# One-core decoder layer with routed experts: the last group's routing, tile tables and scatters spread over more tiles

## The chip, the core and the metric

The kernel runs on one core of one Trainium2 chip. The metric is the time of the whole kernel on the device in microseconds (us), the median of several runs.

## What is computed

Sixteen sequences of 128 tokens with 128 features pass three sublayers, each followed by an addition and a layer norm: a self-attention with circulant projections, a cross attention with a context of 120 rows, and a mixture-of-experts layer. Only the last one matters here. In the reference it is

```python
scores = jax.nn.softmax(xt @ gate_w.T, axis=-1)
_, idx = jax.lax.top_k(scores + gate_b, 2)
...
for each of the 8 experts:
    h = swiglu((xt @ ew1 + eb1) * (xt @ ew3 + eb3))
    routed = routed + ce[:, None] * (h @ ew2 + eb2)
shared = swiglu((xt @ sw1 + sb1) * (xt @ sw3 + sb3)) @ sw2 + sb2
return routed + shared
```

(the loop is a scan in the reference). So each of the 2048 tokens goes to two of eight experts, and to one shared expert.

## The kernel before, in words

**Stages.** The sixteen batches are four groups of four (`NG`, `G4`). A long software pipeline of slots (`front`, slots up to `LAST_SLOT`) does the attentions. For groups 0 to 2 it also does the routing. From iteration m = -1 on a second pipeline runs 47 expert tiles of 128 rows through the experts (`tile`, lines 1471, 845 and 1067): tiles 0 to 7 are the shared expert for the last eight batches, tiles 8 to 23 (`NE` = 16) hold rows of groups 0 to 2 sorted by expert, and tiles 24 to 46 the rest, with the last group's rows in them. From m = 6 on only this tile pipeline is left, and all that is changed lies in it.

**A routed row's way.** GpSimd scatters each token's row twice into the DRAM buffer `xs` at the place `slot` (`scatter`, L628; before the fourth and the eighth batch's half `mark`, L615, writes destination and weight beside the rows). SyncE loads one tile of 128 rows from `xs` into a ring of four buffers (`load`, L471) by an address that it reads from the table `row_of`. TensorE transposes it. The products follow, ScalarE scales the result with the row's weight (L868), and GpSimd places it in the DRAM buffer `ys` (`place`, L706) by destinations that `meta` (L690) took out of the loaded rows. After all tiles `ys` is read back and summed, normed and stored.

**One iteration m of the tile pipeline.** TensorE (L1520, L1551 to L1560) transposes the hidden values of tile m-2 and the input rows of tile m+1 (L1482, L1484), makes the first product of tile m (L1491 into pS), the down product of tile m-2 (L1502 into pM) and the second product of tile m (L1491 into pT). It starts with a wait for the hidden values of tile m-2. VectorE's loop m does whatever routing is due, and then tile m-1: product (L1071), two clips (L1073, L1074), gate (L1076), hidden (L1079). ScalarE copies, takes a tanh and scales the output of tile m-2. GpSimd calls `place(i)` when the output of routed tile i is there, in iteration m = i + 10, then `meta(i + 4)`.

**The last group's routing** is written by hand into VectorE's loops. It has nine steps: 0 the largest logit, 1 softmax and bias, 2 and 3 the first choice, 4 and 5 the second, 6 the weights, 7 first rows (after two small matmuls of counts on TensorE, `counts`, L1359), 8 the slots. Then come `late_tiles` (eleven small instructions) and `tile_table` (seven), which give `expert_of` and `row_of` for tiles 24 to 46. Nearly every one of them goes through `link`, which makes the next one wait for its end. `LAST_ROUTING` names the loop of each step: steps 1 and 2 in loop 7, 3 and 4 in loop 8, 5 in loop 9, 6 and 7 in loop 10, 8 in loop 11. `LAST_COUNT` = 10, `LAST_TILES` = 12, `LAST_TABLE` = 13.

**The last group's scatters** are eight, in two batches of four: behind `place(1)` and `meta(5)`, and behind `place(3)` and `meta(7)` (L722). GpSimd works in order.

**SyncE** loads routed tiles 0 to 15 (numbered r, tile r + 8), each once the ring's buffer is free (`t_ps`, `meta_sb`). Behind `load(9)` (`PAD_LOAD`) it writes eight blocks of padding rows, one for each expert. Then it waits for all eight scatters of the last group, the padding and the second table, and goes on with `load(16)`, which TensorE reads in iteration 23:

```python
sp.wait_ge(s_scat_last, 16 * 2 * G4)
sp.wait_ge(s_pad, 16 * (E + 1))
sp.wait_ge(tab_sb, 2)
for r in range(NE, NR):
    load(r)
```

Of the kernel before, what the change touches and what calls it, by code (L numbers as in the profile page):

```python
# [22 lines left out]
G4 = 4  # L23
NG = B // G4
# [10 lines left out]
NR = (2 * B * P + E * (P - 1)) // P  # L35
NE = (2 * (NG - 1) * G4 * P - E * (P - 1)) // P
# [9 lines left out]
X_SLOTS = {-7: 1, 1: 2, 9: 3}  # L46
BIAS_SLOTS = {7: 0, 11: 1, 15: 2}
SHARED_SLOT, SHARED_SLOTS, SHARED_DOWN = 25, 20, 9
PAD_LOAD = 9
LAST_ROUTING = {6: (0,), 7: (1, 2), 8: (3, 4), 9: (5,), 10: (6, 7), 11: (8,)}  # L50
LAST_COUNT, LAST_TILES, LAST_TABLE = 10, 12, 13
RING = 4
XW = D + 2
CAP = B * P + P
# [13 lines left out]
def decoder_layer(nc, x, ctx_1024, wq_c, wq_b, wk_c, wk_b, wv_c, wv_b, wo_c, wo_b, w_sim, b_sim, W_qv, b_qv,  # L68
# [9 lines left out]
    with ctx:  # L78
# [291 lines left out]
        def scat_sem(g):  # L370
            return s_scat_last if g == NG - 1 else s_scat
# [6 lines left out]
        def _(sp):  # L378
# [92 lines left out]
            def load(r):  # L471

                row = sp.value_load(row_of[0:1, bass.ds(r, 1)], min_val=0, max_val=DUMMY)
                if r >= RING:
                    sp.wait_ge(t_ps, NA + r - RING + 1)
                    sp.wait_ge(meta_sb, r - RING + 1)
                sp.dma_start(XR[:, r % RING, :], xs.ap()[bass.ds(row, P), :]).then_inc(s_load[r % RING], 16)
# [53 lines left out]
            for r in range(NE):  # L531
                load(r)
                if r == PAD_LOAD:
                    sp.wait_ge(pad_sb, 1)
# [26 lines left out]
        def _(pool):  # L561
# [53 lines left out]
            def mark(g, k):  # L615

                if k == 0:
                    pool.wait_ge(slots_sb, g + 1)
                    pool.wait_ge(x2_sb, G4 * (g + 1))
                else:  # L620
                    pool.wait_ge(scat_sem(g), 16 * G4 * (2 * g + 1 if g < NG - 1 else 1))
                rows = X2[:, g * G4:(g + 1) * G4, :]
                pool.tensor_copy(rows[:, :, D:D + 1].rearrange("p b o -> p (b o)"), dest[:, k, g * G4:(g + 1) * G4])
                pool.tensor_copy(rows[:, :, D + 1:D + 2].rearrange("p b o -> p (b o)"),
                                 weight[:, k, g * G4:(g + 1) * G4]).then_inc(marked, 1)
                pool.wait_ge(marked, 2 * g + k + 1)

            def scatter(g, i):  # L628

                k, b = i // G4, g * G4 + i % G4  # L630
                if i % G4 == 0:
                    mark(g, k)
                pool.indirect_dma_start(xs.ap(), bass.IndirectOffsetOnAxis(ap=slot[:, k, b:b + 1], axis=0),  # L633
                                        X2[:, b, :], None).then_inc(scat_sem(g), 16)
# [55 lines left out]
            def meta(i):  # L690

                k = i % (2 * RING)
                pool.wait_ge(s_load[i % RING], 16 * (i // RING + 1))
                if i >= 2 * RING:
                    pool.wait_ge(s_ysc[i % RING], 16 * (i // RING - 1))
                pool.tensor_tensor(row_weight[:, k:k + 1], XR[:, i % RING, D + 1:D + 2], zero[:], ALU.add)
                to = XR[:, i % RING, D:D + 1]
                if i % RING == 0:
                    pool.tensor_copy(row_dest[:, k:k + 1], to).then_inc(meta_sb, 1)
                else:  # L700

                    pool.tensor_scalar(spare[:, k:k + 1], to, 2.0 * TOKENS - 0.5, float(i % RING * P), ALU.is_ge, ALU.mult).then_inc(spare_sb, 1)
                    pool.wait_ge(spare_sb, i - i // RING)
                    pool.tensor_scalar(row_dest[:, k:k + 1], spare[:, k:k + 1], to, None, ALU.add).then_inc(meta_sb, 1)

            def place(i):  # L706

                k = i % (2 * RING)
                pool.wait_ge(y_sb, NA + 1 + i)
                pool.wait_ge(meta_sb, i + 1)  # L710
                pool.indirect_dma_start(ys.ap(), bass.IndirectOffsetOnAxis(ap=row_dest[:, k:k + 1], axis=0),  # L711
                                        YO[:, i % RING, :], None).then_inc(s_ysc[i % RING], 16)
# [5 lines left out]
            for i in range(NR):  # L718
                place(i)
                if i + RING < NR:  # L720
                    meta(i + RING)
                if i in (1, 3):  # L722
                    for k in range(G4):
                        scatter(NG - 1, (i // 2) * G4 + k)
            for g in range(NG):
                here = slice(g * G4, (g + 1) * G4)
                mean, var = (meanvar3[:, here, i:i + 1].rearrange("p b o -> p (b o)") for i in range(2))
# [11 lines left out]
        def _(act):  # L739
# [153 lines left out]
            for m in range(LAST_SLOT - FFN_SLOT + 1, NT + 2):  # L893
                if 0 in LAST_ROUTING.get(m, ()):
                    route_exp(NG - 1)
# [11 lines left out]
        def _(dve):  # L907
# [176 lines left out]
            def link(ins):  # L1084

                steps_done[0] += 1
                ins.then_inc(rt, 1)
                dve.wait_ge(rt, steps_done[0])
# [69 lines left out]
            def first_tiles():  # L1158

                link(dve.tensor_tensor_scan(tiles_cum[:], ones[:, 0:E], tiles[:], 0.0, ALU.mult, ALU.add))  # L1160
                link(dve.tensor_tensor(total[:], tiles_cum[:], tiles[:], ALU.subtract))
                link(dve.memset(start[:, E:E + 1], float(DUMMY)))
                link(dve.scalar_tensor_tensor(out=start[:, 0:E], in0=total[:], scalar=float(-P), in1=region[:], op0=ALU.mult, op1=ALU.add))
# [7 lines left out]
                link(dve.tensor_scalar(used[:], used[:], 0.0, None, ALU.max))  # L1171
                link(dve.tensor_tensor(step[:], start[:, 1:E + 1], start[:, 0:E], ALU.subtract))

            def late_tiles():

                round_tiles((P - 1) / (2.0 * P))
                link(dve.tensor_tensor(tiles[:], tiles[:], used[:], ALU.subtract))
                first_tiles()
                link(dve.scalar_tensor_tensor(out=start[:, 0:E], in0=used[:], scalar=float(P), in1=start[:, 0:E], op0=ALU.mult, op1=ALU.add))
                link(dve.tensor_tensor(step[:], start[:, 1:E + 1], start[:, 0:E], ALU.subtract))  # L1180

            def tile_table(first, n):


                link(dve.tensor_tensor(past[:, 0:n], iota_t[:, 0:n].rearrange("p (t o) -> p t o", o=1).to_broadcast([1, n, E]),
                                       bass.AP(tiles_cum, 0, [[E, 1], [0, n], [1, E]]), ALU.is_ge))
                link(dve.tensor_reduce(out=tab_f[:, 0:n], in_=past[:, 0:n], axis=AX.X, op=ALU.add))
                link(dve.tensor_scalar(expert_of[:, NA + first:NA + first + n], tab_f[:, 0:n], float(E - 1), None, ALU.min))
                link(dve.tensor_tensor(past_step[:, 0:n], past[:, 0:n], bass.AP(step, 0, [[E, 1], [0, n], [1, E]]), ALU.mult))
                link(dve.tensor_reduce(out=row_f[:, 0:n], in_=past_step[:, 0:n], axis=AX.X, op=ALU.add))  # L1190
                link(dve.scalar_tensor_tensor(out=row_f[:, 0:n], in0=row_f[:, 0:n], scalar=start[0:1, 0:1], in1=iota_rows[:, 0:n],
                                              op0=ALU.add, op1=ALU.add))
                dve.tensor_scalar(row_of[:, first:first + n], row_f[:, 0:n], float(DUMMY), None, ALU.min).then_inc(tab_sb, 1)
# [36 lines left out]
            for n in range(FIRST_SLOT, LAST_SLOT + 1):  # L1230
                if n == PREP_SLOT:
                    dve.wait_ge(s_small, 16 * SMALL)
                    for q in range(4):
                        context(q)
                front(n)
                for g in range(NG - 1):
                    if n == G4 * U * g + ROUTE_SLOT and g == 0:
                        dve.wait_ge(c_pool, 4)
                    routing(g, n - G4 * U * g - ROUTE_SLOT)
                if shared_use(n - 1):  # L1240
                    shared_products(*shared_use(n - 1))
                if shared_use(n - 2):
                    shared_hidden(*shared_use(n - 2))
                if n == EARLY_TILES:
                    early_tiles()
                if n == EARLY_TILES + 1:
                    tile_table(0, NE)
                if n >= FFN_SLOT + 1:
                    tile(n - FFN_SLOT - 1, (n - FFN_SLOT - 1) % 2)
            for m in range(LAST_SLOT - FFN_SLOT + 1, NT + 1):  # L1250

                for k in LAST_ROUTING.get(m, ()):
                    routing(NG - 1, k)
                    if k == LATE_COUNT + 1:
                        padding_rows()
                if m == LAST_TILES:
                    late_tiles()
                if m == LAST_TABLE:
                    tile_table(NE, NR - NE)
                tile(m - 1, (m - 1) % 2)  # L1260
            for g in range(NG):
                final_stats(g)
# [338 lines left out]
```

## Time and profile before

| what | us |
|---|---|
| median of 3 runs | 420.73 |
| lowest and highest of them | 417.86, 422.58 |
| the profiled execution | 423.07 |
| its span, first to last instruction | 421.3 |

The rows below are of the profiled execution. Times are from the start of its span. PE is TensorE's matmul, DVE is VectorE, ACT ScalarE, POOL GpSimd, SPq the issuing of SyncE. A name such as L1482 is a line of the kernel before. A bracket at the end of a row gives the idle time before it and what ended it. The first iteration of the tile pipeline whose transposed rows come from `xs` (shown as sim_add) is iteration 7; the L1482 row then marks the start of each iteration.

### The profile page before, as it was taken

The page shows a single profiled execution, that of the slowest core. Times are in us where ns is not written, and L with a number is a line of the kernel's source. Part 1 is how long each engine was busy: PE and PEld are TensorE (multiplying, and loading weights), DVE is VectorE, ACT ScalarE, POOL GpSimd, SP SyncE. Part 2 cuts the span into 40 slices and gives each one's busy share as a digit, 9 for nine tenths or more (in the row PEclk, how much of TensorE's full clock was granted, in tenths as well). Part 3 has the DMA queues.
Part 4 walks back from the last instruction along what each step waited for, and adds up shares of the span by engine and source line. Part 5 has one row for each costly group of instructions (what it writes and reads, how often), then busy time and mean ns, then how long its engine had stood idle before and what let it go on. Part 6 is the DMA issues. An engine that isn't in the chain of part 4 may idle for free.

```text
span 421.3 us, 8518 instructions
## 1 busy us (share of the span) xinstructions
PE 347.6 (82%) x2415; PEld 224.6 (53%) x2415; DVE 281.5 (67%) x834; ACT 175.3 (42%) x498; POOL 194.0 (46%) x377
## 2 busy tenths in 40 slices
PE   2637887888988879798967998978799999999880
PEld 1224466666656658576656554534455555555450
DVE  3435477777878897869876867987466666666322
ACT  2212344444534443344532344344355555555313
POOL 9700022224222558722474434357755656565323
PEclk9999999998999998969998799999899999999996
DMA  4764544766654732310003001113211111110063
GB/s 100 171 212 128 178 141 120 210 202 172 186 157 132 201 98 63 104 34 11 27 28 119 14 13 44 33 39 92 63 45 44 47 45 45 40 50 19 26 201 100
DMA packets 53197, 39.56 MB, mean 94 GB/s; under 512 B 7623, under 2 KB 46632, under 8 KB 53147
## 3 DMA queue, kind: packets, MB, share of 16 engines
q1 hardware_dynamic: 50881, 34.33, 29.3%
q0 software_dynamic: 2272, 4.69, 3.3%
q8 instruction: 22, 0.36, 0.4%
q14 instruction: 22, 0.18, 0.1%
HBM read 26.05 MB, written 12.69 MB: 92 GB/s over the span
## 4 chain that ended last, share of the span: by engine, by line
PE 42%; DVE 23%; issue 10%; POOL 9%; DMA 6%; SPq 5%; ACT 2%; ACTq 0%; POOLq 0%; DVEq 0%
PE pT L1491 7%; PE pS L1491 6%; DVE negmax L934 4%; PE pM L1502 4%; POOL xs L633 3%; PE pM L1297 3%; DVE inv_den L950 2%; POOL rstd L613 2%; PE pO L1482 2%; PE pT L1321 2%; PE pT L1492 2%; PE pS L1311 2%; PE pS L1492 2%; PE pO L1334 2%; DVE X L1004 1%
## 5 line engine op out<-in xcount | busy, mean ns | idle before, releaser
L711 POOL DMA_INDIRECT ys<-sim_rhs,row_dest x39 | 40.5, 1039 | 43.3 <-ACT sim_rhs L868 41.7
L766 ACT ACTIVATE PT<-pT 128x512 f32<-128x512 f32 x64 | 38.0, 594 | 33.3 <-PE pT L1321 29.9
L1491 PE MATMUL pT<-W,XH 128*128 (+1 forms) x94 | 51.7, 632 | 0.0
L934 DVE TENSOR_REDUCE negmax<-pS 128x4 f32<-128x512 f32 x64 | 43.4, 679 | 9.6 <-PE pS L1311 9.2
L1071 DVE TENSOR_TENSOR PT<-pT,PT 128x512 f32<-128x512 f32 x47 | 32.4, 689 | 25.9 <-PE pT L1492 17.7
L1491 PE MATMUL pS<-W,XH 128*128 (+1 forms) x94 | 49.3, 607 | 0.0
L611 POOL TENSOR_SCALAR vareps<-meanvar 128x1 f32<-128x1 f32 x32 | 8.4, 263 | 86.1 <-DVE meanvar L963 85.8
L1311 PE MATMUL pS<-Kdiag,Qst 128*128 128x512 f32 x64 | 40.4, 638 | 6.3 <-DMA Kdiag<-parts_scr 4.7
L852 ACT COPY XH<-pO 128x384 f32<-128x384 f32 x47 | 22.4, 478 | 49.4 <-PE pO L1484 45.7
L1502 PEld LDWEIGHTS pM<-W,XH 128*128 128x128 f32 x188 | 28.1, 191 | 21.0 <-issue 17.4
L633 POOL DMA_INDIRECT xs<-X,slot x32 | 33.2, 1036 | 8.1 <-issue 5.8
L1321 PE MATMUL pT<-Qdiag,Kst 128*128 128x512 f32 x64 | 31.0, 485 | 1.8 <-DMA Qdiag<-maxT 1.2
L1502 PE MATMUL pM<-W,XH 128*128 (+1 forms) x188 | 29.0, 277 | 3.8 <-ACT XH L852 3.8
L654 POOL TENSOR_TENSOR hq_x<-X1T,hqT 128x128 f32<-128x128 f32 x16 | 7.3, 457 | 49.4 <-ACT hqT L787 49.4
L1076 DVE SCALAR_TENSOR_TENSOR Vz<-Vz,XT 128x256 f32<-128x256 f32 x47 | 20.0, 425 | 13.6 <-ACT Vz L855 12.8
L858 ACT COPY PT<-pS 128x512 f32<-128x512 f32 x47 | 27.3, 581 | 2.9 <-PE pS L1492 2.8
L1334 PE MATMUL pO<-PT,Vz 128*32 128x128 f32 x512 | 27.9, 292 | 0.0
L855 ACT ACTIVATE Vz<-XT 128x256 f32<-128x256 f32 x47 | 19.6, 417 | 18.6 <-DVE XT L1073 18.3
L1338 PE MATMUL pO<-PT,head_ones 128*32 128x128 f32 x512 | 27.1, 286 | 0.0
L1482 PEld LDWEIGHTS pO<-ident,hid 128*128 128x128 f32 x94 | 12.7, 145 | 25.2 <-issue 18.6
L1482 PE MATMUL pO<-ident,hid 128*128 128x128 f32 x94 | 18.6, 280 | 6.6 <-issue 4.2
L1311 PEld LDWEIGHTS pS<-Kdiag,Qst 128*128 128x128 f32 x64 | 13.9, 221 | 13.5 <-issue 13.4
(264 smaller groups left out, 828.1 us busy)
## 6 DMA issues: line engine op xcount, KB each, us to landing
parts_scr<-qk_hi SPq DMA_DIRECT2D x16, 256.0 KB, 2.9
W<-in_L_ffn_w SPq DMA_DIRECT2D x16, 256.0 KB, 3.9
Qst<-parts_scr SPq DMA_DIRECT2D x32, 96.0 KB
Kdiag<-parts_scr SPq DMA_DIRECT2D x64, 48.0 KB
Kst<-parts_scr SPq DMA_DIRECT2D x32, 96.0 KB
Qdiag<-parts_scr SPq DMA_DIRECT2D x64, 48.0 KB
sim_add<-xs SPq DMA_DIRECT2D x39, 65.0 KB
parts_scr<-qk_lo SPq DMA_DIRECT2D x8, 256.0 KB, 3.0
```

Source lines behind the costliest of these rows:

```text
L633: pool.indirect_dma_start(xs.ap(), bass.IndirectOffsetOnAxis(ap=slot[:, k, b:b + 1], axis=0), X2[:, b, :], None).then_inc(scat_sem(g), 16)
L711: pool.indirect_dma_start(ys.ap(), bass.IndirectOffsetOnAxis(ap=row_dest[:, k:k + 1], axis=0), YO[:, i % RING, :], None).then_inc(s_ysc[i ...
L766: act.activation(PT[:, u % 3, :], pT[:, 0, :], ACT.Exp, scale=SCALE).then_inc(p_sb, 1)
L858: act.copy(up1[:, p, :], pS[:, p, :]).then_inc(up1_sb, 1)
L934: dve.tensor_reduce(out=negmax[:, b % 2, HG * j:HG * (j + 1)], in_=pS[:, u % 2, :].rearrange("p (g k) -> p g k", g=HG), axis=AX.X, op=ALU.max,
L1071: dve.tensor_tensor(prod[:, p, :], pT[:, p, :], up1[:, p, :], ALU.mult).then_inc(prod_sb, 1)
L1311: pe.matmul(pS[:, u % 2, :], Qst[:, (b // 2) % 2, j, (b % 2) * P:(b % 2 + 1) * P], Kdiag[:, b % 2, j, :, :], start=True, stop=True).then_i ...
L1321: pe.matmul(pT[:, 0, :], Kst[:, (b // 2) % 2, j, (b % 2) * P:(b % 2 + 1) * P], Qdiag[:, b % 2, j, :, :], start=True, stop=True).then_inc(s ...
L1334: pe.matmul(pO[32 * hg:32 * hg + 32, 0:P], Vz[:, b % 2, hg, j, :], PT[:, u % 3, hg * P:(hg + 1) * P], start=(j == 0), stop=(j == U - 1), s ...
L1482: mm = pe.transpose(pO[:, k * P:(k + 1) * P], hid[:, p, k * P:(k + 1) * P], ident[:])
L1491: pe.matmul(bank, XH[:, 1 - p, 2 * P:3 * P], W[:, bass.ds(e_up * I2, I2)], start=True, stop=False)
L1502: pe.matmul(pM[:, 0:D], XH[:, p, k * P:(k + 1) * P], W2[:, bass.ds(e_y * I + k * D, D)], start=(k == 0), stop=False)
```

## The change

The nine steps go to eight loops, with only 4 and 5 together. The count matmuls move from iteration 10 to 11. `late_tiles` is cut in two (`late_counts` and `late_tiles`) and `tile_table` in two (`tile_experts` and `tile_rows`), for loops 14, 15, 16 and 17. The early table still has its two halves one behind the other. The padding rows move from behind `load(9)` to behind `load(11)`. The eight scatters go one behind each of `place(4)` to `place(9)`, and two behind `place(10)`.

```diff
-PAD_LOAD = 9
-LAST_ROUTING = {6: (0,), 7: (1, 2), 8: (3, 4), 9: (5,), 10: (6, 7), 11: (8,)}
-LAST_COUNT, LAST_TILES, LAST_TABLE = 10, 12, 13
+PAD_LOAD = 11
+LAST_ROUTING = {6: (0,), 7: (1,), 8: (2,), 9: (3,), 10: (4, 5), 11: (6,), 12: (7,), 13: (8,)}
+LAST_COUNT, LAST_TILES = 11, 14
+LAST_SCATTER = {4: (0,), 5: (1,), 6: (2,), 7: (3,), 8: (4,), 9: (5,), 10: (6, 7)}
...
-                if i in (1, 3):
-                    for k in range(G4):
-                        scatter(NG - 1, (i // 2) * G4 + k)
+                for k in LAST_SCATTER.get(i, ()):
+                    scatter(NG - 1, k)
...
-            def late_tiles():
+            def late_counts():
 
                 round_tiles((P - 1) / (2.0 * P))
                 link(dve.tensor_tensor(tiles[:], tiles[:], used[:], ALU.subtract))
+
+            def late_tiles():
+
                 first_tiles()
                 link(dve.scalar_tensor_tensor(out=start[:, 0:E], in0=used[:], scalar=float(P), in1=start[:, 0:E], op0=ALU.mult, op1=ALU.add))
                 link(dve.tensor_tensor(step[:], start[:, 1:E + 1], start[:, 0:E], ALU.subtract))
 
-            def tile_table(first, n):
+            def tile_experts(first, n):
...
                 link(dve.tensor_scalar(expert_of[:, NA + first:NA + first + n], tab_f[:, 0:n], float(E - 1), None, ALU.min))
+
+            def tile_rows(first, n):
+
                 link(dve.tensor_tensor(past_step[:, 0:n], past[:, 0:n], bass.AP(step, 0, [[E, 1], [0, n], [1, E]]), ALU.mult))
...
                 if m == LAST_TILES:
+                    late_counts()
+                if m == LAST_TILES + 1:
                     late_tiles()
-                if m == LAST_TABLE:
-                    tile_table(NE, NR - NE)
+                if m == LAST_TILES + 2:
+                    tile_experts(NE, NR - NE)
+                if m == LAST_TILES + 3:
+                    tile_rows(NE, NR - NE)
```

## Rows read from the trace of the kernel before

**Rows 1.** The page: busy time, share of the span and instructions of the engines.

```profile
PE 347.6 (82%) x2415; PEld 224.6 (53%) x2415; DVE 281.5 (67%) x834; ACT 175.3 (42%) x498; POOL 194.0 (46%) x377
```

**Rows 2.** Timeline of PE: start, duration, line, output and inputs, idle time before.

```profile
261.47 0.44 PE L1482 MATMUL pO<-ident,hid 128*128 128x128 f32 x2 [1.17 <-DMA sim_add<-xs]
...
276.14 0.41 PE L1482 MATMUL pO<-ident,hid 128*128 128x128 f32 x2 [1.27 <-issue]
...
297.33 0.38 PE L1482 MATMUL pO<-ident,hid 128*128 128x128 f32 x2
...
298.52 0.38 PE L1492 MATMUL pS<-bias,bias_rows 128*128 x1
301.39 0.71 PE L1502 MATMUL pM<-W,XH 128*128 x4 [2.49 <-ACT XH L852]
...
301.99 2.00 PE L1491 MATMUL pT<-W,XH 128*128 x2
...
307.84 0.38 PE L1482 MATMUL pO<-ident,hid 128*128 128x128 f32 x2
...
310.87 0.38 PE L1482 MATMUL pO<-ident,hid 128*128 128x128 f32 x2
```

**Rows 3.** Timeline of DVE in loops 8, 10, 12, 13 and two later ones.

```profile
265.11 0.69 DVE L1071 TENSOR_TENSOR PT<-pT,PT 128x512 f32<-128x512 f32 x1
...
270.88 1.20 DVE L1126 TENSOR_TENSOR picked_of<-pick,rexp 128x64 f32<-128x64 f32 x1
...
273.67 0.68 DVE L1071 TENSOR_TENSOR PT<-pT,PT 128x512 f32<-128x512 f32 x1
...
279.04 0.16 DVE L1152 TENSOR_TENSOR total<-first_row,region 128x8 f32<-128x8 f32 x1
...
281.25 0.69 DVE L1071 TENSOR_TENSOR PT<-pT,PT 128x512 f32<-128x512 f32 x1
...
283.56 0.33 DVE L1185 TENSOR_TENSOR past<-iota_t,tiles_cum 1x184 f32<-1x184 f32 x1
...
285.58 0.68 DVE L1071 TENSOR_TENSOR PT<-pT,PT 128x512 f32<-128x512 f32 x1
...
300.57 0.69 DVE L1071 TENSOR_TENSOR PT<-pT,PT 128x512 f32<-128x512 f32 x1 [3.60 <-remote]
...
323.21 0.69 DVE L1071 TENSOR_TENSOR PT<-pT,PT 128x512 f32<-128x512 f32 x1 [0.65 <-issue]
```

**Rows 4.** Timeline of POOL: the last group's first scatters, placings, and one free iteration.

```profile
281.74 1.08 POOL L633 DMA_INDIRECT xs<-X,slot  x1 [0.28 <-POOL X L624]
...
285.66 0.96 POOL L633 DMA_INDIRECT xs<-X,slot  x1 [0.30 <-issue]
286.92 0.95 POOL L711 DMA_INDIRECT ys<-sim_rhs,row_dest  x1 [0.30 <-issue]
...
288.52 0.29 POOL L704 TENSOR_SCALAR row_dest<-spare,sim_add 128x1 int32<-128x1 f32 x1
...
295.81 0.96 POOL L633 DMA_INDIRECT xs<-X,slot  x1 [0.30 <-issue]
...
325.76 1.07 POOL L711 DMA_INDIRECT ys<-sim_rhs,row_dest  x1 [0.90 <-ACT sim_rhs L868]
```

**Rows 5.** The chain of waits: group 2's last scatter and the first load behind it.

```profile
256.34 2.27 DMA xs<-X,slot
...
259.62 1.80 DMA sim_add<-xs
```

**Rows 6.** Timeline of SyncE: the load before the padding rows, and the two after.

```profile
281.41 0.34 SPq L477 DMA_DIRECT2D sim_add<-xs  x1
...
293.94 2.20 SPq L477 DMA_DIRECT2D sim_add<-xs  x2
```

**Rows 7.** Windows: stretch, length, busy time by engine, PEclk, DMA share, GB/s.

```profile
298.60:302.00 3.40, 0.91 (x8) 0.60 (x6) 1.25 (x3) 1.12 (x4) 2.53 (x5) 1.00 0.27 76
302.00:305.40 3.40, 3.40 (x9) 1.78 (x8) 1.76 (x5) 1.08 (x4) 2.73 (x7) 0.50 0.15 41
```

More of the change, by code:

```diff
@@ L1246, in _ @@
                 if n == EARLY_TILES + 1:
-                    tile_table(0, NE)
+                    tile_experts(0, NE)
+                    tile_rows(0, NE)
                 if n >= FFN_SLOT + 1:
```

## The prediction

> **What bounds the kernel now.** I read the page's busy times first: TensorE is busy for 82% of the span, VectorE for 67% [rows 1]. That is an average over two pipelines, so I went to the timeline of TensorE in the stretch that is changed, and took the start of each iteration (its L1482 row). Far from the routing an iteration takes 310.87 - 307.84 = 3.03 us with no idle time [rows 2]: there TensorE is the bound. From iteration 7 (261.47) to iteration 19 (307.84) there are twelve iterations in 46.37 us, where 12 x 3.03 = 36.4 would do. Some 10 us are lost, in two parts.
>
> The first, up to iteration 17 at 297.33, is 297.33 - 261.47 - 10 x 3.03 = 5.5 us. It is VectorE's. A tile without routing keeps it busy for 3.03 - 0.65 = 2.38 us (the bracket at 323.21) [rows 3]. Routing of length x ahead of a tile makes the loop 2.31 + x (2.31 since the wait for the tanh shrinks a little), which is more than TensorE's 3.03 once x is over 0.72. Loops 10, 12 and 13 have x = 273.67 - 270.88 = 2.79, 2.21 and 2.02 [rows 3].
>
> The second part is 4.5 us, from iteration 17 to 19: 307.84 - 297.33 is 10.51, two iterations are 6.07. TensorE had its matmuls in the trace by 298.9 (298.52 + 0.38), yet VectorE (300.57, after 3.60 idle, "remote") and ScalarE went on only at 300.5, and TensorE at 301.39 [rows 2, 3]. I find no row that explains this pause; I come back to it. Behind it the granted clock is 0.50 of full, which is 1.2 GHz, from 302.0 to 305.4, after a stretch in which TensorE was busy for 0.91 of 3.40 us [rows 7], and two pT matmuls take 2.00 us [rows 2]. Half a clock for 3.4 us costs a TensorE-bound stage 1.7.
>
> **VectorE's part of the change.** No instruction is added or removed, only moved. A link costs 0.20 to 0.22 us: eleven from 279.04 to 281.25, and seven larger ones from 283.56 to 285.58, 0.29 each [rows 3]. By these, x per new loop is: loop 7 (4 links) 0.87, loop 8 (3) 0.67, loop 9 (3) 0.66, loop 10 (6) 1.22, loop 11 (3) 0.71, loop 12 (6) 1.10, loop 13 (4) 0.79, loop 14 (5) 1.03, loop 15 (6) 1.18, loop 16 (3) 0.93, loop 17 (4) 1.09. A single overrun of some 0.35 is swallowed, since hidden values are ready that much before TensorE asks.
>
> One long instruction is not a link's size: L1126 took 1.20 at 270.88 where its like takes about 0.2 [rows 3]. GpSimd was adding the shared output at that time, in both kernels at the same point of the pipeline, so I keep 1.0 us for it in loop 10 and 0.6 to 0.8 in loop 9, where the first such addition lies.
>
> Loop by loop from 261.47 (that start waits for the first load and stays), iteration 11 comes at 275.7 (before 276.14), 12 at 278.8, 13 at 282.3, 14 at 285.4, 15 at 288.8, 16 at 292.4, 17 at 295.7 and 18 at 299.2. So VectorE's part gains 297.33 - 295.7 = 1.6 us at iteration 17, and gives 0.4 of it back in loop 17, the last: 1.2 us. Between 0 (if the links stall more often beside GpSimd) and 3.5 (if all overruns are swallowed) I take 1.2, which is nearest to the rows. The count matmuls (0.36 us) run while TensorE waits for loop 9's tile, now as free as an idle slot. Without further waits, iteration 19 is then at 302.2 and iteration 23 at 302.2 + 12.1 = 314.35.
>
> **GpSimd's part.** Here is the cost. In a free iteration GpSimd has 0.90 us to spare (the bracket at 325.76) [rows 4]. A scatter takes 0.96 + 0.30, more than that. Placing and `meta` back to back take 1.89 (286.92 to 288.52 + 0.29); with 0.28 ahead of the scatter, 0.96 of it and 0.30 behind, an iteration with one scatter takes 3.45 us of GpSimd, and by estimate 3.7 if `meta`'s small instructions run slower beside VectorE's. With `mark` ahead and the short `meta`, it is about 3.26. TensorE's is 3.03 to 3.4, so from `place(6)` on GpSimd is never idle and falls behind. A placing comes 325.76 - 323.21 = 2.55 us after the tile product of its loop [rows 3, 4]; `place(5)` is then at 289.9 + 2.5 = 292.4, and the starts are: `place(6)` 295.85, `place(7)` 299.3, `place(8)` 302.8, `place(9)` 306.1, `place(10)` 309.6, the last scatter 313.1.
>
> Its lateness hurts only one thing. `place` and `meta` have four tiles of ring, 12.1 us, and the lag is under 4. But SyncE waits for all eight scatters before it issues `load(16)`, and TensorE needs those rows in iteration 23. From the start of group 2's last scatter (256.34) to the transposition of the rows loaded behind it (261.47) it took 5.1 us: 2.27 to land, 1.0 for the wait and the address, 1.8 for the load [rows 2, 5]. So `load(16)` is there at 313.1 + 5.1 = 318.2, and TensorE, due at 314.35, waits 3.8 us. The bounds are 1.5 (placings 0.3 us quicker each, earlier output) and 5.5 (3.7 per iteration). I take 3.8. Before, this cover was large: the last scatter started at 295.8 [rows 4] and the load was not due until iteration 19.
>
> A stop of that length is longer than the one behind which the clock fell to 1.2 GHz [rows 2, 7]; I add the same 1.7 us. The Trainium skill ("TensorE: Matmul & The Clock Gate", What's actually happening) says that the clock halves after an idle stretch and returns after a busy one; with its rule read strictly, a stop that isn't a whole such stretch costs nothing and the sum is 1.7 us lower. The rows speak against the strict reading, since 0.91 us of work in 3.40 did not save the clock.
>
> **SyncE's part.** Eight paddings and their addresses cost 293.94 - 281.41 = 12.5 us from load to load [rows 6]. Behind `load(11)`, free at about 287.6 when `meta(7)` is done, `load(12)` is issued at about 300.3 and there at 301.8, with iteration 19 asking at 302.2. That margin of 0.4 us is thin: 0 is taken, 1 us is its price, and the stop at iteration 23 would absorb most of it, as GpSimd's chain doesn't wait for it by then.
>
> The Trainium skill ("SBUF — State Buffer", Who interferes with whom) has a rule that speaks against scatters among tiles: GpSimd writes its descriptors through a port that VectorE's two-port instructions lock. If it held here at full size each scatter would be longer by up to a clip. In the rows the scatter beside tile work takes 0.96 to 1.08 and the placing 1.07 [rows 4], so it is worth 0.1 us each at most, and I leave it out.
>
> **The sum.** Iteration 23 starts at 318.2, and 1.7 us of slow clock bring it to the equal of 319.9. Before it was at 307.84 + 12.13 = 319.97. So the change is -0.1 us against the profiled execution: 423.07 - 0.1 = 423.0. The routing's gain and the pause of before are both swallowed by one new wait. The median of the runs, 420.73, is 2.3 below the profiled one; a part of the runs may lack the pause. A run of this kernel tells a change from none at about 1%, 4.2 us.
>
> **Rivals.**
> 1. The pause of 296.4 to 300.5 isn't in most runs, only in the profiled one. For it: it has no cause in the rows, and the lowest run is 417.86, about 423.07 - 4.5 = 418.6. Against it: the highest is 422.58. Then nothing is given back. The late `load(16)` costs 318.2 + 1.7 - (307.84 - 4.45 + 12.13 = 315.5) = 4.4, on top of 420.73: 425.1, slower. It decides from the point where the wait in iteration 23 is longer than what loops 7 to 17 gave, 1.2 us.
> 2. GpSimd keeps up, by a quicker placing or a later TensorE, and `load(16)` comes in time. Against it: 0.90 us of room for 1.26 of work. Then 423.07 - 4.5 - 1.2 = 417.4, and with the pause kept 421.9.
> 3. The padding rows make `load(12)` late by over 1 us, and GpSimd's placings shift with it: 426.
>
> **Chances.** The forecast 0.50; rival 1 0.25; rival 2 0.20; rival 3 0.05. Bounds of 1% around 420.73 are 416.5 and 424.9. Faster: half of rival 2 and a little of the rest, 0.13. Slower: most of rivals 1 and 3, and the upper edge of the forecast, 0.30. Within: 0.57. The range, 417.4 to 426.2, takes in both other sides; the forecast's own is 421 to 425.
>
> **What would show it.** In the changed profile, loops of 2.31 + x on VectorE, none above 4.6 us; GpSimd without idle time ahead of `place(7)` to `place(10)`; the last scatter near 313; TensorE idle in iteration 23, released by the load of sim_add from xs, for 3 to 5 us, and a granted clock of 0.50 behind it. The prediction is wrong if the last scatter starts before 309.3, or if iteration 23 has no wait.

## The result, and the profile after

The changed kernel takes 424.07 us (median of 6, 420.92 to 425.66), the kernel before 420.09 (median of 6, 417.86 to 422.58). The ratio is 1.0088, with a 95% interval of 1.0046 to 1.013: slower by 0.9%, or 4.0 us, inside the range and within 1%. In a later session the same two gave 423.42 against 424.47, a ratio of 0.998 (0.994 to 1.002); the section on the pause comes back to the two times of the kernel before, whose cause stays open.

The timeline of TensorE in the changed kernel follows. L1492 is the old L1482; the rows are iterations 7, 17, 19, 22, 23, 24 and 25, with the last product ahead of the stop. They answer to [rows 2].

```profile
259.52 0.44 PE L1492 MATMUL pO<-ident,hid 128*128 128x128 f32 x2 [1.23 <-DMA sim_add<-xs]
...
293.15 0.41 PE L1492 MATMUL pO<-ident,hid 128*128 128x128 f32 x2 [0.32 <-issue]
...
299.62 0.38 PE L1492 MATMUL pO<-ident,hid 128*128 128x128 f32 x2
...
308.72 0.38 PE L1492 MATMUL pO<-ident,hid 128*128 128x128 f32 x2
...
311.54 0.38 PE L1502 MATMUL pT<-bias,bias_rows 128*128 x1
...
316.12 0.44 PE L1492 MATMUL pO<-ident,hid 128*128 128x128 f32 x2 [4.20 <-DMA sim_add<-xs]
...
320.88 0.38 PE L1492 MATMUL pO<-ident,hid 128*128 128x128 f32 x2
...
323.91 0.38 PE L1492 MATMUL pO<-ident,hid 128*128 128x128 f32 x2
```

The start of iteration 7 depends on all that lies ahead of it and moves by 3 us from execution to execution (259.75 to 262.83 in four profiles of the kernel before, here 259.52), so I count from it. Up to iteration 17 the changed kernel takes 33.63 us, before 35.86: the routing gained. Iteration 23 then waits 4.20 us for rows of `xs`, and the next one takes 4.76 us instead of 3.03. From iteration 7 to 27, twenty iterations on, it is 70.46.

The timeline of GpSimd answers to [rows 4]: `place(5)` to `place(10)` without the scatters between them, the last two scatters, and `place(11)`.

```profile
289.61 1.00 POOL L712 DMA_INDIRECT ys<-sim_rhs,row_dest  x1 [0.58 <-ACT sim_rhs L868]
...
293.15 0.99 POOL L712 DMA_INDIRECT ys<-sim_rhs,row_dest  x1 [0.32 <-ACT sim_rhs L868]
...
296.71 0.96 POOL L712 DMA_INDIRECT ys<-sim_rhs,row_dest  x1 [0.30 <-issue]
...
300.53 0.96 POOL L712 DMA_INDIRECT ys<-sim_rhs,row_dest  x1 [0.30 <-issue]
...
303.96 0.97 POOL L712 DMA_INDIRECT ys<-sim_rhs,row_dest  x1 [0.30 <-issue]
...
307.53 1.12 POOL L712 DMA_INDIRECT ys<-sim_rhs,row_dest  x1 [0.30 <-issue]
...
309.74 1.15 POOL L634 DMA_INDIRECT xs<-X,slot  x1 [0.16 <-issue]
311.19 0.96 POOL L634 DMA_INDIRECT xs<-X,slot  x1 [0.31 <-issue]
312.45 0.96 POOL L712 DMA_INDIRECT ys<-sim_rhs,row_dest  x1 [0.30 <-issue]
```

From `place(7)` (296.71) on nothing but the fixed 0.30 stands ahead of a placing: GpSimd is the bound of its own queue. Placings come 3.4 to 3.8 us apart, TensorE's iterations 3.03 to 3.55. The chain of waits shows how its last scatter ends up on TensorE; it answers to [rows 5].

```profile
311.19 2.29 DMA xs<-X,slot
313.48 0.02 issue
313.49 0.28 SPq L474
...
314.28 1.79 DMA sim_add<-xs
316.07 0.04 issue
316.12 0.44 PE pO L1492 x2
```

From the scatter's start to TensorE's are 4.93 us. The windows ahead of the stop's end, behind it, and one iteration on answer to [rows 7]: no matmul for 4.1 us, then a granted clock of 0.64 on average over 4.7 us, and full clock again. With only the two levels of 1.2 and 2.4 GHz, 0.64 is about 3.4 of the 4.7 us at the lower one.

```profile
312.00:316.10 4.10, 0.00 (x0) 0.00 (x0) 1.14 (x3) 0.00 (x0) 2.91 (x6) 1.00 0.17 48
316.10:320.80 4.70, 4.68 (x14) 2.73 (x15) 0.85 (x2) 1.75 (x4) 0.57 (x3) 0.64 0.30 71
320.80:323.90 3.10, 3.10 (x16) 1.78 (x15) 2.04 (x5) 1.70 (x4) 2.01 (x5) 1.00 0.06 21
```

### The profile page after: what moved, and what is told of

Same layout as the page of the kernel before. It is cut to its first block, busy times and chain, and to the rows that moved or that the text cites. A ratio compares the mean times of both kernels' runs of the same rounds, so it can differ in the third digit from the quotient of the medians.

```text
span 419.2 us, 8518 instructions
## 1 busy us (share of the span) xinstructions
PE 346.0 (83%) x2415; PEld 222.8 (53%) x2415; DVE 281.2 (67%) x834; ACT 175.0 (42%) x498; POOL 195.3 (47%) x377
## 4 chain that ended last, share of the span: by engine, by line
PE 41%; DVE 25%; POOL 11%; issue 10%; DMA 6%; SPq 3%; ACT 2%; POOLq 0%; ACTq 0%; DVEq 0%
PE pT L1501 6%; PE pS L1501 6%; DVE negmax L934 4%; PE pM L1512 3%; PE pM L1307 3%; POOL xs L634 2%; DVE inv_den L950 2%; POOL rstd L614 2%; POOL ys L712 2%; PE pT L1331 2%; PE pO L1492 2%; PE pO L1344 2%; DVE stats L961 2%; PE pS L1502 1%; DMA X<-in_x 1%
## 5 line engine op out<-in xcount | busy, mean ns | idle before, releaser
L1501 PE MATMUL pT<-W,XH 128*128 (+1 forms) x94 | 50.6, 620 | 0.0
L1331 PE MATMUL pT<-Qdiag,Kst 128*128 128x512 f32 x64 | 30.1, 471 | 2.7 <-DMA Qdiag<-maxT 2.3
L1492 PEld LDWEIGHTS pO<-ident,hid 128*128 128x128 f32 x94 | 12.1, 143 | 27.6 <-issue 16.4
L1492 PE MATMUL pO<-ident,hid 128*128 128x128 f32 x94 | 18.5, 278 | 8.6 <-DMA sim_add<-xs 5.4
L1079 DVE SCALAR_TENSOR_TENSOR hid<-XT,Vz 128x256 f32<-128x256 f32 x47 | 20.0, 424 | 1.6
```

The costliest lines, as they stand in the source:

```text
L1331: pe.matmul(pT[:, 0, :], Kst[:, (b // 2) % 2, j, (b % 2) * P:(b % 2 + 1) * P], Qdiag[:, b % 2, j, :, :], start=True, stop=True).then_inc(s ...
L1492: mm = pe.transpose(pO[:, k * P:(k + 1) * P], hid[:, p, k * P:(k + 1) * P], ident[:])
L1501: pe.matmul(bank, XH[:, 1 - p, 2 * P:3 * P], W[:, bass.ds(e_up * I2, I2)], start=True, stop=False)
```

## The experiments

Two theories stand against each other at first. A: the loss is the wait for rows that the last scatter holds back. B: the spread routing, or scatters among the tiles as such, cost the time.

**The routing alone.** The scatters in two batches of four again, as early as the later slots allow.

```diff
-LAST_SCATTER = {4: (0,), 5: (1,), 6: (2,), 7: (3,), 8: (4,), 9: (5,), 10: (6, 7)}
+LAST_SCATTER = {3: (0, 1, 2, 3), 5: (4, 5, 6, 7)}
```

> The spread routing with the scatters left in two batches of four, behind place(3) and place(5). Theory A (the loss is the wait for rows behind the last scatter): the last scatter starts near 299, load(16) is in time, iteration 23 has no wait on xs, and the time is 4 to 6 us below the changed kernel, 1 us below the kernel before (about 419). Theory B (the spread routing itself, or its place, costs): the time stays at 423 to 425 though the wait in iteration 23 is gone.

Measured: 417.54 us, ratio to the kernel before 0.995 (0.9915 to 0.9985). No wait in iteration 23, and iterations 7 to 27 in 64.21 us. A profile of the kernel before from the same session took 66.50 there (shown in the section on the pause). B falls for the routing: it is the gain, 2.3 us.

**The scatters alone.** The kernel before with the changed kernel's `LAST_SCATTER` (its line is left out here) and the loop that reads it.

```diff
-                if i in (1, 3):
-                    for k in range(G4):
-                        scatter(NG - 1, (i // 2) * G4 + k)
+                for k in LAST_SCATTER.get(i, ()):
+                    scatter(NG - 1, k)
```

> The routing and tables of before, with the eight scatters one behind each placed tile, the last two behind place(10). Theory A: the last scatter starts near 313 again, TensorE waits 2.5 to 4 us in iteration 23 for rows of xs, and the time is 3 to 5 us over the kernel before (423 to 425). Theory B: no loss, 420.

Measured: 427.31 us (median of four), ratio 1.0197 (1.0133 to 1.026), iterations 7 to 27 in 73.62. TensorE's timeline in iteration 23:

```profile
320.77 0.69 PE L1482 MATMUL pO<-ident,hid 128*128 128x128 f32 x2 [4.95 <-DMA sim_add<-xs]
```

The last scatter started at 315.89, 54.2 us behind iteration 7 where the changed kernel has 51.7: by the old routing iteration 7 to 17 takes 36.0 us, and the placings follow. So the loss, 7.5 us, is more than the 3 to 5 that I wrote, with the stop at 4.95 and 2.4 us of slow clock behind it. A stands, its size was low.

**Scatters in pairs, from the earliest placing on.** They are among the tiles as in the change, but early.

```diff
-LAST_SCATTER = {4: (0,), 5: (1,), 6: (2,), 7: (3,), 8: (4,), 9: (5,), 10: (6, 7)}
+LAST_SCATTER = {3: (0, 1), 4: (2, 3), 5: (4, 5), 6: (6, 7)}
```

> The changed kernel with two scatters behind each of place(3), (4), (5) and (6), so that the last starts near 301. Theory A: no wait in iteration 23, and 1 to 2 us below the kernel before (419). Theory B (scatters among tiles hold up the tiles wherever they stand): 423 or more.

Measured: 416.91 us, ratio 0.9939 (0.9907 to 0.997), iterations 7 to 27 in 63.99, last scatter at 301.82. B falls for the scatters too: among the tiles they cost nothing as long as the last is early. Timed again,

> The version with two scatters behind each of place(3) to place(6), timed again. Where the kernel before has its pause and takes 424.5 us, the ratio should be near 0.983 (its own time stays at 417); where it has not and takes 420, near 0.994. A time of its own above 420 would mean that the pause can befall it too.

it took 417.25 against 420.91, ratio 0.9928 (0.9893 to 0.9962).

**One tile earlier, one later.** The whole row of scatters is moved by one placing, so the last two stand behind `place(9)` or `place(11)`.

```diff
-LAST_SCATTER = {4: (0,), 5: (1,), 6: (2,), 7: (3,), 8: (4,), 9: (5,), 10: (6, 7)}
+LAST_SCATTER = {3: (0,), 4: (1,), 5: (2,), 6: (3,), 7: (4,), 8: (5,), 9: (6, 7)}
...
+LAST_SCATTER = {5: (0,), 6: (1,), 7: (2,), 8: (3,), 9: (4,), 10: (5,), 11: (6, 7)}
```

> The changed kernel with every scatter one tile earlier, the last two behind place(9). If the stop in iteration 23 is set by the last scatter alone, that scatter starts about 3.5 us earlier, 48 us behind iteration 7, the rows are there 53.2 behind it against TensorE's 51.9, so the stop is 1 to 1.5 us instead of 4.2 and the clock may stay at full: 3 to 5 us below the changed kernel, 419 to 421. If something else stops TensorE there, the wait stays at 4 us.

> Every scatter one tile later, the last two behind place(11). If the last scatter alone sets the stop, it starts about 3.4 us later than in the changed kernel and the stop grows from 4.2 to 7.6 us: 427 to 428. If GpSimd's lag is what counts, it hardly moves.

Measured: 418.53 us and 426.80 us. Iteration 23 of the earlier one:

```profile
313.77 0.44 PE L1492 MATMUL pO<-ident,hid 128*128 128x128 f32 x2 [1.39 <-DMA sim_add<-xs]
```

and of the later one:

```profile
321.85 0.69 PE L1492 MATMUL pO<-ident,hid 128*128 128x128 f32 x2 [8.16 <-DMA sim_add<-xs]
```

The last scatter starts 48.3, 51.7 and 55.7 us behind iteration 7, and iteration 23 starts 53.25, 56.60 and 60.77 us behind it: it follows the scatter one for one, 4.9 to 5.1 us after its start. The stop itself is 1.39, 4.20 and 8.16 us. It grows by a little less (2.8 for 3.35, 4.0 for 4.17), since TensorE comes to it 0.3 and then 0.4 us later. Behind the short stop the clock stays at full (iteration 23 to 24 takes 3.09 us), so the step from 4.20 to 1.39 is worth 70.46 - 65.44 = 5.0 us from iteration 7 to 27, and more than the stop alone. The runs of the kernel before beside these took 424.54 us, so the ratios to it (0.9864 and 1.0049) mislead. The medians of the kernels themselves are compared here, across sessions: the changed kernel took 424.07 and 423.42 in two others.

**The clock's share.** Sixteen spare matmuls whose result isn't used, ahead of TensorE's wait. The two waits in front of them, long met by then, keep them from writing over values in `pX` that are still to be read.

```diff
+                if m == NA + NE - 1:
+                    pe.wait_ge(cnt_sb, NG)
+                    pe.wait_ge(lg_sb, B)
+                    for _ in range(FILL):
+                        pe.matmul(pX[:, 0, 0:D], ones[:], ones[:], start=True, stop=True)
```

> The changed kernel with 16 spare matmuls (about 4.2 us of work whose result is not used) ahead of TensorE's wait in iteration 23. If 1.7 us of the loss are the clock at 1.2 GHz behind the stop, the granted clock stays at full there, iteration 23 to 24 takes 3.03 us instead of 4.76, and the time is 1.7 us below the changed kernel (422.4). If the clock has nothing to do with it, the time is that of the changed kernel, 424.

Measured: 422.52 us, against 424.07 and 423.42 of the changed kernel in other sessions, so the times agree with a gain of 0.9 to 1.6 us without fixing it. Iterations 7 to 27 take 68.89 us, against 70.46. In its timeline of TensorE the spare work, the rest of the wait, and the next iteration are

```profile
317.29 3.73 PE L1573 MATMUL pX<-ones 128*128 128x128 f32 x32
321.67 0.44 PE L1493 MATMUL pO<-ident,hid 128*128 128x128 f32 x2 [0.65 <-DMA sim_add<-xs]
...
324.77 0.38 PE L1493 MATMUL pO<-ident,hid 128*128 128x128 f32 x2
```

and its windows beside and behind them

```profile
315.00:321.60 6.60, 5.97 (x42) 4.85 (x41) 2.68 (x8) 1.48 (x4) 5.01 (x8) 1.00 0.13 40
321.60:324.80 3.20, 3.13 (x15) 1.88 (x16) 0.85 (x2) 1.66 (x4) 0.62 (x3) 1.00 0.31 83
```

The granted clock stays at 1.00, and iteration 23 to 24 takes 3.10 us, not 4.76. In that profile the rows come as late as in the changed kernel (iteration 23 is 56.69 us behind iteration 7, there 56.60). So of the loss in iteration 23 and behind it, 1.7 us are the clock and 4.2 the wait. The Trainium skill ("TensorE: Matmul & The Clock Gate", What's actually happening) has the clock fall behind idleness; these two kernels agree, with the same wait for rows and the fall only where TensorE was idle through it.

**Nine loops for nine steps.** Steps 4 and 5 apart as well, with the tables, the padding and the pairs of scatters one place later.

```diff
-LAST_ROUTING = {6: (0,), 7: (1,), 8: (2,), 9: (3,), 10: (4, 5), 11: (6,), 12: (7,), 13: (8,)}
-LAST_COUNT, LAST_TILES = 11, 14
+LAST_ROUTING = {6: (0,), 7: (1,), 8: (2,), 9: (3,), 10: (4,), 11: (5,), 12: (6,), 13: (7,), 14: (8,)}
+LAST_COUNT, LAST_TILES = 12, 15
...
+PAD_LOAD = 12
+LAST_SCATTER = {4: (0, 1), 5: (2, 3), 6: (4, 5), 7: (6, 7)}
```

> Steps 4 and 5 too in loops of their own, tables one loop later, padding behind load(12), scatters in pairs behind place(4) to place(7). The last scatter starts some 45 us behind iteration 7, still ahead of the 46.7 that the rows need, so there should be no stop. VectorE's overrun in loop 10 falls by 0.5 us. Expected 0.3 us below the version with pairs from place(3) on, iteration 7 to 27 in 63.7 us; if some other wait limits those loops, no change at 64.0.

Measured: 417.34 us; iterations 7 to 27 in 63.78 against 63.99 of the pairs. Iteration 11 comes 0.56 us earlier (13.15 against 13.71), as expected of loop 10, but only 0.2 of it, and of the 0.3 that I had forecast, is left at the end. The times (416.91 and 417.25 for the pairs) can't tell it from none.

## The pause in the kernel before

> The kernel before, profiled once more. If the pause of 4 us near iteration 17 belongs to the kernel, it stands in this profile too, and iterations 7 to 19 take 46.4 us again. If it was an accident of one execution, they take about 42 us, and the clock stays at full there.

This profile had no pause: iteration 7 to 19 in 42.23 us, 7 to 27 in 66.50, the clock at full there, and 416.89 us. I took it for an accident. But in the next session the kernel before took 424.54 us, while the versions made from the change kept to 417 and 418. So two more profiles:

> The kernel before under a label of its own, timed against itself. In the last call it took 424.5 us, in the two calls ahead 420, while the other kernels kept their times. If a session or chip decides, this run and the shared runs agree with each other, at 420 or at 424.5. If it is 424.5, the profile shows whether the 4.5 us are the pause near iteration 17 (iterations 7 to 19 in 46.4 us) or lie elsewhere (42.2 us).

> A third profile of the kernel before, for how often the pause occurs: 42.2 us from iteration 7 to 19 without it, 46.4 with it.

Both have it: iterations 7 to 19 in 46.49 and 46.53 us, 7 to 27 in 70.76 and 70.80; timed against itself the kernel gives 424.28 and 424.47. The timelines of TensorE and of VectorE in the profile of `before_third` show the same picture as [rows 2, 3]:

```profile
297.80 0.38 PE L1482 MATMUL pO<-ident,hid 128*128 128x128 f32 x2
...
298.99 0.38 PE L1492 MATMUL pS<-bias,bias_rows 128*128 x1
301.75 0.71 PE L1502 MATMUL pM<-W,XH 128*128 x4 [2.38 <-ACT XH L852]
```

```profile
300.92 0.69 DVE L1071 TENSOR_TENSOR PT<-pT,PT 128x512 f32<-128x512 f32 x1 [3.49 <-remote]
```

So the pause is no accident of one execution. It comes at the same iteration of the kernel before and costs 4.1 to 4.3 us with its clock (46.37 to 46.53 against 42.23). The kernel's medians were 419.85 and 420.91 us in two sessions and 424.54 and 424.47 in two others; the sessions at 419.85 and 424.54 ran on the same chip, so it isn't the chip. The session on record lies between, with the pause in its profile (423.07) and a median of 420.09. That a whole session runs with the pause or without it is read from these medians, not shown by profiles. None of ten profiles of versions with the spread routing or the moved scatters had it, five of them from the sessions at 424.5. What it is stays open: TensorE's matmuls are in the trace before it, yet those who wait for them go on 3.5 us later, and no row names a cause. It isn't the loading of instructions: in the three profiles with the pause, the DMA queues for instructions moved nothing from 290 to 305 us.

> The changed kernel once more. Its wait in iteration 23 sits behind everything in the loops ahead, so its time should not depend on a pause there: 423 to 425, with 4.2 us of stop and iterations 7 to 27 in 70.5 us. If it rises with the kernel before in a slow session, the session's extra lies outside those loops.

Measured: 423.42 us, a stop of 4.15 us, and 70.43 from iteration 7 to 27: the changed kernel's own time is nearly the same in both kinds of session.

## Why the prediction was right

**The steps.** Each is counted from the start of iteration 7.

| step | predicted | measured |
|---|---|---|
| iteration 17 | 34.2 | 33.63 |
| iteration 19 | 40.7 | 40.10 |
| last scatter starts | 51.6 | 51.67 |
| scatter to the transposed rows | 5.1 | 4.93 |
| iteration 23 | 56.7 | 56.60 |
| stop in iteration 23 | 3.8 | 4.20 |
| clock behind it | 1.7 | 1.73 |

So the place, the mechanism and the size of the new wait were right. The fill run and the shifted scatters show what it is made of, and wait and clock account for all of it: against the routing alone, iteration 23 comes 4.52 us later (56.60 against 52.08, the stop of 4.20 and 0.3 ahead of it) and the next one takes 1.73 more, together the 6.25 by which 70.46 is over 64.21.

That the last scatter came within 0.1 us of the forecast is luck. `place(5)` came 30.09 us behind iteration 7 where I had 30.9, and from there to `place(10)` the placings were 3.58 apart where I had 3.44; the two errors cancel. The scatters took up to 1.15 us among the tiles where I had counted 0.96.

Padding: `load(12)` was issued at 295.42 in the changed profile, 35.9 us behind iteration 7, where I had 38.8; and with 1.8 us to land the rows were there 2.4 us ahead of iteration 19, not 0.4. From load to load the paddings took 10.3 us where [rows 6] had 12.5, as these rows of SyncE show (`load(11)`, the first padding; the last padding, `load(12)`). Rival 3 had no ground.

```profile
285.09 0.34 SPq L478 DMA_DIRECT2D sim_add<-xs  x1
286.22 0.37 SPq L538 DMA_DIRECT2D xs<-pad_row  x1
...
294.27 0.33 SPq L538 DMA_DIRECT2D xs<-pad_row  x1
295.42 0.36 SPq L478 DMA_DIRECT2D sim_add<-xs  x1
```

**VectorE's term was too small.** I gave the routing 1.2 us. The routing alone gains 66.50 - 64.21 = 2.3 in the profiles and 2.3 in the medians. Most loops came out within 0.1 us of 2.31 + x, as loop 15, the one with `late_tiles`, shows (283.58 to 287.12, 3.54, for 2.31 + 1.18). Loop 16 was longer, 3.49 for 2.31 + 0.93. At iteration 19 it is 42.23 - 40.10 = 2.1, where I had 41.9 - 40.7 = 1.2. Of the 0.9 between them, 0.3 is the base, since I had priced the pause at 4.5 us and it is 4.2. The other 0.6 is in the loops: loop 10, which I had charged with the full 1.0 us of the stalled L1126, has its product starts 4.28 apart (266.46 to 270.74) instead of 4.53. The stall came in that loop, but on another instruction: L1110 took 0.96 us beside GpSimd's addition, where its like takes 0.2. By iteration 11 TensorE is 0.5 us ahead of the forecast (13.70 against 14.2); what brought the part of it that isn't loop 10's was not singled out.

**The sum, and which base.** I set the change against the profiled execution, pause and all, and got -0.1 us. Against a kernel before with the pause this is right: 70.46 against 70.64 from iteration 7 to 27, and 423.42 against 424.47 in a session with the pause. Against a kernel before without it the cost is 70.46 - 66.50 = 4.0 us, and the medians on record (424.07 - 420.09 = 4.0) fit that case, though the one profile of that session has the pause. This is rival 1, for which I had worked out 4.4 and given one chance in four. So the step of the forecast that did not hold is that the pause of before is given back: in the medians on record nothing is. That the time still came out within 1.1 us of 423.0 is no proof of the sum, since the forecast stood on the profiled execution, which already held the pause; and that the change stayed within 1% is close to luck, as 4.0 us is 0.95% of 420.09 and rival 1 as worked out would have been over it. The hint was in the table: the profiled execution was slower than the highest of its three runs.

**Rival 2**, GpSimd keeping up, didn't happen: nothing but the fixed 0.30 stands ahead of its placings from `place(7)` on. What it would have given, no wait in iteration 23 and 417.4 us, is what the pairs give in another way (416.91), since their last scatter is early.

## What to carry to other kernels

Spreading work on a queue that is in order delays its last piece by everything in between. Ask who waits for the last piece, and by when, before asking what each piece costs: here the spread routing (nobody waits for it until late) gained 2.3 us, the spread scatters (all eight gate one load) cost 6.3 (70.46 - 64.21). When a profiled execution is slower than the runs beside it, take a second profile before its odd gap is made a term of the sum.

## What was not expected of the hardware

A stop of 1.39 us left TensorE's clock at 2.4 GHz. A stop of 4.20 brought 1.2 GHz and 1.7 us behind it, one of 4.95 brought 2.4 us (scatters alone), and one of 8.16 only 2.1 (iteration 23 to 24 in 5.09). In the last two the granted clock was at 0.50 already in the last part of the stop (from 319.00 to 320.70, and from 320.00 to 321.80), so a part of the slow clock cost nothing there; in the first it was at 1.00 until the stop's end. 3.73 us of work without use in the gap kept it at 2.4. And the same program has a pause of 4.1 to 4.3 us with its clock, at one fixed place, in three of four profiles. No profile of a version with work moved by a few iterations had it; that the move took it away is likely from that, and not shown.
